# Attention's joint product and the relation features' way into PSUM: one stacked product for two, transposes for products

## The reference, cut to what matters

```python
# layer 1
z = feature @ W_out + b_out
e = gelu(s_src[src] + s_dst[dst])            # scores from z and attn_w
a = softmax of e over the edges of one dst   # segment max, exp, segment sum
h = segment_sum(a[:, None] * z[src], dst) + (feature @ res_W + res_b)
# layer 2
proj = einsum('ni,rio->nro', nfeat, relation_weight)
t_r, h_r = proj[src, etype], proj[dst, etype]
att = sum(t_r * tanh(h_r + efeat), axis=-1)  # efeat: edge_attr_64
a = softmax of att over the edges of one dst
h_nb = segment_sum(nfeat[src] * a[:, None], dst)
out = leaky((nfeat + h_nb) @ res_fc_w.T) + leaky(nfeat * h_nb @ res_fc2_w.T)
```

## Time and profile before

| | us |
|---|---|
| median of three runs | 5169.54 (5166.43 to 5170.01) |
| the profiled execution | 5170.97 |
| its span, first to last instruction | 5169.1 |
| attention, 2104 to 2796 us of the span | 692 |
| relations, 2796 to 4140 us | 1344 |
| messages, 4140 us to the end | 1029 |
| PE busy in the span | 4409.3 (85%) |
| VectorE busy | 3315.3 (64%) |
| POOL busy | 2830.7 (55%) |
| ScalarE busy | 1901.1 (37%) |

### The profile page before, as it was taken

One profiled execution on the slowest core, in us unless ns is written; L12 is line 12 of the kernel. 1 busy time (PEld: TensorE's weight loads), 2 busy tenths in 40 slices (PEclk: granted clock), 3 DMA queues, 4 the chain that ended last, 5 costly groups with the idle time before them and its releaser, 6 DMA issues. The chain is left out here.

```text
span 5169.1 us, 80284 instructions
## 1 busy us (share of the span) xinstructions
PE 4409.3 (85%) x25341; PEld 3022.9 (58%) x25341; DVE 3315.3 (64%) x6849; ACT 1901.1 (37%) x3531; POOL 2830.7 (55%) x2859
## 2 busy tenths in 40 slices
PE   5989998999989999579987898989898767777765
PEld 1278886888877777246666455555555444444433
DVE  9967776676656666567766688888888633333332
ACT  0056665444434444112121144545454422222222
POOL 0066664776645555576632544444443067777777
PEclk9989999999989999766665998989899688988898
DMA  1089997899956665345433433434343132222221
GB/s 37 1 249 286 287 288 227 221 233 231 230 153 164 166 165 159 85 97 121 115 76 74 98 94 91 100 86 101 93 95 78 34 79 64 65 54 64 65 64 30
DMA packets 1124520, 649.11 MB, mean 126 GB/s; under 512 B 907542, under 2 KB 940589, under 8 KB 1124104
## 3 DMA queue, kind: packets, MB, share of 16 engines
q1 hardware_dynamic: 1036296, 555.84, 39.3%
q0 software_dynamic: 87808, 88.16, 8.7%
HBM read 384.69 MB, written 261.63 MB: 125 GB/s over the span
## 5 line engine op out<-in xcount | busy, mean ns | idle before, releaser
L2183 POOL DMA_INDIRECT r_got<-x_table,slot_idx x392 | 430.3, 1098 | 752.2 <-DVE r_both_t L2407 320.5
L1056 POOL DMA_INDIRECT o_rows<-in_x_dram,dst_idx x392 | 370.6, 945 | 467.6 <-POOLq L347 265.5
L1507 POOL DMA_INDIRECT b_rows<-h_table,slot_idx x392 | 369.5, 943 | 291.1 <-DVE n_power L1012 122.1
L2498 POOL DMA_INDIRECT m_rows<-x_table,slot_idx x392 | 376.1, 959 | 235.7 <-issue 118.8
L1962 POOL DMA_INDIRECT t_got<-x_table,slot_idx x392 | 385.7, 984 | 189.2 <-issue 109.4
L2637 DVE TENSOR_TENSOR_SCAN m_both<-m_keep,m_both,m_rows_t 128x512 f32<-128x512 bf16 x97 | 124.1, 1280 | 562.6 <-PE m_rows_t L2560 562.6
L1318 POOL DMA_INDIRECT a_got<-node_table,src_idx x392 | 375.8, 959 | 194.2 <-DVE a_conv L1454 56.0
L2282 PE MATMUL r_source_t<-r_masked,rel_pair 64*128 64x512 f32 x980 | 468.9, 624 | 0.0
L2284 PE MATMUL r_own_t<-r_masked,rel_pair 64*128 64x512 f32 x980 | 468.8, 624 | 0.0
L2506 POOL DMA_INDIRECT out_dram<-s_res,put_out x392 | 390.6, 996 | 137.2 <-issue 113.1
L1012 DVE TENSOR_REDUCE n_power<-n_square 128x8 f32<-128x512 f32 x294 | 200.5, 682 | 384.4 <-ACT n_square L987 381.2
(11 more groups left out here) (401 smaller groups left out, 12502.6 us busy)
## 6 DMA issues: line engine op xcount, KB each, us to landing
x_table<-n_res SPq DMA_DIRECT2D x196, 256.0 KB
n_rows<-x_table SPq DMA_DIRECT2D x196, 256.0 KB, 3.4
x_table<-s_res SPq DMA_DIRECT2D x294, 128.0 KB
node_table<-n_wide SPq DMA_DIRECT2D x98, 272.0 KB, 4.0
h_table<-n_conv SPq DMA_DIRECT2D x98, 256.0 KB, 3.9
x_table<-s_res SPq DMA_DIRECT2D x98, 256.0 KB
r_feats<-in_edge_attr_dram SPq DMA_DIRECT2D x390, 64.0 KB
n_rows<-in_x_dram SPq DMA_DIRECT2D x97, 256.0 KB, 3.8
```

What stands on the lines that cost most here:

```text
L1056: nc.gpsimd.indirect_dma_start(out=rows[:, n % 4, t, :], out_offset=None, in_=x, in_offset=bass.IndirectOffsetOnAxis(ap=dst_idx[:, n * TIL ...
L1507: nc.gpsimd.indirect_dma_start(out=rows[:, n % 4, t, 0:D], out_offset=None, in_=h_table, in_offset=bass.IndirectOffsetOnAxis(ap=slot_idx[: ...
L2183: nc.gpsimd.indirect_dma_start(out=got[:, n % RING, t, :], out_offset=None, in_=x2_table, in_offset=bass.IndirectOffsetOnAxis(ap=slot_idx[ ...
L2498: nc.gpsimd.indirect_dma_start(out=rows[:, n % 4, t, 0:D], out_offset=None, in_=x3_table, in_offset=bass.IndirectOffsetOnAxis(ap=slot_idx[ ...
```

## The change

In attention, a new step lift on ScalarE copies a block's scanned weighted rows (lower partitions of place b + X) into the lower partitions of place b of the ring, beside its own rows. It waits for that scan and stands behind roots and ahead of squares in ScalarE's turn. The weights of both are stacked into one tile, w_out_res. So add_up has one product a tile, and it waits for lift in place of the scan. In the relation phase the products of the features with the identity become transposes (is_transpose), into the same bank and with products added onto them as before.

```diff
-    w_out_cen = sb(ctx, "w_out_cen", [P, D])
+    w_out_res = sb(ctx, "w_out_res", [P, D])
...
-                vec.memset(w_out_cen[:, :], 0.0).then_inc(*v.one())
...
-                vec.tensor_scalar(w_out_cen[0:D, :], w_out2[0:D, :], scores[0:D, 1:2], None, ALU.add).then_inc(*v.one())
+                vec.tensor_scalar(w_out_res[0:D, :], w_out2[0:D, :], scores[0:D, 1:2], None, ALU.add).then_inc(*v.one())
+                vec.tensor_scalar(w_out_res[D:P, :], res2[D:P, :], scores[D:P, 2:3], None, ALU.add).then_inc(*v.one())
...
+            lifted = sig.get("lifted")
...
                     def add_up(b):
-                        n = b + X
-                        pe.wait_ge(scanned[n], scanned.done(n))
+                        pe.wait_ge(lifted[b], lifted.done(b))
...
                         for t in range(TILES):
-                            k = slice(t * P, (t + 1) * P)
-                            nc.tensor.matmul(to[:, t, :], scan[:, n % SCANS, k], w_out_cen[:, :], start=False, stop=False,
-                                             skip_group_check=True)
-                            last = nc.tensor.matmul(to[:, t, :], scan[:, b % SCANS, k], res_pair[:, 1, :], start=False, stop=True,
-                                                    skip_group_check=True)
+                            last = nc.tensor.matmul(to[:, t, :], scan[:, b % SCANS, t * P:(t + 1) * P], w_out_res[:, :], start=False,
+                                                    stop=True, skip_group_check=True)
...
+                    def lift(b):
+                        act.wait_ge(scanned[b + X], scanned.done(b + X))
+                        nc.scalar.activation(scan[0:D, b % SCANS, :], scan[0:D, (b + X) % SCANS, :], ACT.Copy).then_inc(lifted[b], 1)
...
-                    over_turns((roots, X + 3, BLOCKS), (squares, X + 2, BLOCKS), 
+                    over_turns((roots, X + 3, BLOCKS), (lift, X + 1, BLOCKS), (squares, X + 2, BLOCKS),
                                soft.after(3, keep_chunk, act), soft.after(7, soft.weigh, act))
...
                             nc.tensor.matmul(own_t[:, t * P:(t + 1) * P], feats[:, n % 3, t].rearrange("p k d -> p (k d)"), ident[:, :],
-                                             start=(t == 0), stop=False, skip_group_check=True)
+                                             start=(t == 0), stop=False, is_transpose=True, skip_group_check=True)
```

## The result

| | before | after |
|---|---|---|
| median, us | 5167.99 (4 runs, 5165.22 to 5170.01) | 5096.36 (4 runs, 5092.74 to 5098.3) |
| the profiled execution | 5170.97 | 5095.01 |
| its span | 5169.1 | 5093.3 |

The account below looks back on a forecast made before the run. PE was busiest, at 85% of the span, but taken as the bound only in stretches where it sets a turn's end. Attention -50 and relation -34 made -84: 5169.5 - 84 = 5086 us, range 5065 to 5125.

Parts of the forecast that it names:

- Slow turns of attention: Attention's middle, five turns per softmax chunk at 1.2 GHz: 1.6 us less each, 8.0 in all.
- The Exp turn: Attention's middle, one turn per chunk: the square waits for scan and copy, Exp work queues behind it, 2.2 us more.
- Three turns in which PE runs without a gap: Attention's middle, per chunk, one at 1.2 GHz and two at 2.4: PE's saving shortens them, 2.9 us less.
- Turns at 2.4 GHz: Attention's middle, five turns per chunk counted with others where VectorE is busy: 0.15 us more each, +0.8 in all.
- the first rival: Attention's clock stays at 1.2 GHz in turns that now reach 2.4, PE having less to do: 5106 us, chance 0.24.
- The cut for POOL: Attention's middle: gathers run only four turns ahead, 71 us a chunk, so -35 us taken instead of -41.
- The tail: Attention's last turns: thirteen steady turns fall from 4.38 to 3.55 us, -10, and the dozen before them give -5.
- The price of the transposes: Relation stage: four transposes for four f32 products take 0.45 to 0.55 us less a turn; 0.48 taken.
- the third rival: Relation stage: a transpose into PSUM that is added to costs as much as the product: 5120 us, chance 0.09.
- Seventy turns of it: Relation stage: the scan waits for PE in 70 of 98 turns, each gaining 0.48 us: -34, bounds -44 and -15.
- the fourth rival: 24 relation turns starting at 1.2 GHz: without the products the projection stays at 1.2, +103 us: 5189, chance 0.05.
- a falling clock in either stage: Sign of being wrong: the granted clock of attention or relation falls; relation was to stay at 0.91.

Follow-up runs that it names:

- the seventh experiment: Kernel after with ScalarE's copy lift moved behind the squares and softmax pieces of its turn: 5078.54 us, ratio 0.983.
- the second experiment: Kernel after with the relation features' products put back, so attention's change alone: 5113.43 us, ratio 0.9892.
- the clock held: Kernel after with 3, 1 and 5 extra zero products in PE's idle relation stretches: 5035.36 us; the same with features' products instead of transposes: 5069.61 us.
- the first experiment: Kernel before with the relation transposes alone, without attention's change: 5144.66 us, ratio 0.9941, six runs from 5121.44 to 5153.69.
- the third experiment: Kernel after with each of the relation features' transposes made twice, eight instructions as before: 5107.57 us, ratio 0.9882.

## Why the prediction was right or wrong, point by point

- **Slow turns of attention: right.** 1.6 us each was forecast, 1.7 came (7.14 to 5.45, 6.52 to 4.81, 8.46 to 6.78, 12.07 to 10.37). The waits of power for the square in the middle are gone altogether (under 20 us was the mark).
- **The Exp turn: right.** +2.2 forecast, +2.1 measured; the seventh experiment shows that it was the copy's place.
- **Three turns in which PE runs without a gap: less than forecast.** -2.9 was forecast; -1.8 came, if they are 5.59 to 3.68, 4.11 to 4.67 and 3.92 to 3.47 in the table.
- **Turns at 2.4 GHz: right in size**, 3.39 to 3.47 where 0.15 more was forecast. In one turn of some chunks (4.11 to 4.67) the clock now rises later, the first rival on a small scale; over the middle the granted clock rose.
- **The cut for POOL: the step that failed in attention.** I had -41 for the middle and took -35. It gave -42.9. (The 415 us that I divided by 73 turns hold fewer of them: from scan 25 to scan 98 it is 426.5 us, 82 a chunk and not 80.) The gathers did become the next limit, as their waits show, but at 73 to 75 us a chunk, hardly above the 72 of my uncut sum, which already stood above POOL's 71. The limit was costed rightly and then counted once more.
- **The tail: right**, 3.46 us a turn for 3.55 forecast, -16.7 for -15, at a clock that stayed low. The chain is scan, copy, square, as worked out.
- **Not in the sum:** -2.5 us between the last scan of attention and the first of relations, and -1.0 ahead of the middle. With these and the cut, -50 became -63 in the profiled execution and, in the second experiment, -56 by the ratio and -61 by the medians: at or past the low bound.
- **The price of the transposes: right.** 0.48 us was taken, 0.50 measured in plain turns (10.46 to 9.96); the third rival, a transpose that costs as much as a product, is refuted by the timeline.
- **Seventy turns of it: the step that failed in the relation stage.** Two errors. The 70 waits of the scan for PE are five in a seven, but with the clock held only four remain: the wait of the fifth turn is there because PE runs at 1.2 GHz in it. And one plain turn in three gives just 0.24 us: there PE waits for POOL's pair product, in the whole stage 31.4 us where it was 13.5.

```profile
PE f_score_t L2294 <- POOL r_pair L2193: 31.4, 46, 2.1
```

With the clock held that makes 25 us, not 34.

- **The clock: the rest of that step.** I counted 0.48 us for the turns that start at 1.2 GHz, on the ground that the clock rises in mid-projection. They grew, by 0.87 and 0.38 us. The longer time at the lower level is what the fourth rival had foreseen, at a quarter and a tenth of the 3.5 us from which it decides: it did not make the kernel slower, but in the steady sevens it took the whole gain. The holding of the clock shows the low clock as cause (82.0 against 88.7 us a seven). Why the lower level lasts longer there is open: a longer idle stretch ahead and less work behind don't settle it, as the first experiment had both and 3.41 us at the lower level. I had also named a falling clock in either stage as a sign of being wrong, and it came: 0.88 for 0.89 between the first and the last relation scan, 0.88 for 0.90 in the steady sevens. (The sixteen products of add_up that I set against this rival are sixteen instructions, eight products.)
- **The rule that I weighed**, of the Trainium skill, "TensorE: Matmul & The Clock Gate", Part 4 (PE-mode transpose): transposes don't count as work that lifts the clock. By it the third experiment's fifth turn should have stayed long; it came back from 14.55 to 13.64 us, and eight transposes in a turn left the granted clock at 0.90, as eight instructions of products did. That speaks against the rule for these transposes, among the other products of their turn, but weakly: the same turn took 12.63 us with four.
- **The total** came out 10 us from the forecast (the two parts were off by 13 in one direction and by 21 in the other). A right sum from wrong terms: only the cuts by stage told.

## What to carry to other kernels

Taking work from TensorE in a stage where it idles at times can go with a lower granted clock, which then takes the saving back in other turns (and in another execution not all of it): compare the same turn in both traces, those that wait on a low clock above all, and count as waits on PE only those that remain with the clock up. Filling an idle stretch with idle products of the right length, worked out from their measured duration, brought more (some 60 us) than the transposes had (13 to 30). A step that is put ahead of others in an engine's order makes them wait for all that it waits for; look for the place behind them first.

## What the runs showed of the hardware

- PE idle for 2.4 to 4.5 us ahead of a turn was followed, in the turns shown, by stretches of 3.41 to 10.24 us at 1.2 GHz, in a stage that is otherwise at 2.4; with extra products in these gaps whole sevens ran at a granted clock of 1.00. Per seven, that is worth 6.7 us of 88.7.
- The same program ran 5121 to 5154 us in the first experiment, and the profiled execution of it had sevens of 85.2 and of 88.9 us: the differences are in where the clock is low.
- Four f32 transposes took half the time of the four f32 products that they replace (1.06 against 2.02 us, in the fifth turns of after and before, at 1.2 GHz). Eight of them left the granted clock of a steady seven at 0.90, where the products had it.
- The steady sevens settled at 88.7 us (before, after, attention alone, the copy behind the squares) or at 85.4 (the relation part alone), not at lengths that follow the work taken out.
- ScalarE's copy of 64x512 f32 within SBUF took 0.63 us in all 98 turns, as the earlier trace rows had it.
